# Three paired tiles at every sixth place instead of four at every fourth, with the input turned and the second half gathered earlier in each tile

## The reference, cut to what matters

```python
gate = softmax(x @ gate_w + gate_b)
topv, topi = top_k(gate, 2)                    # two of 8 experts per token
topv = topv / topv.sum(-1)
for e in range(8):
    h = relu(x @ w1[e] + b1[e])                # 256 -> 1024
    y = h @ w2[e] + b2[e]                      # 1024 -> 256
    out += y * combine[:, e]
x = layernorm(x + out)
```

## Time and profile before

| | |
|---|---|
| median of 3 runs | 1365.9 us (1363.53 to 1366.03) |
| profiled execution | 1366.0 us, of which the span from first to last instruction is 1364.2 us |
| granted TensorE clock | 0.996 of full speed |
| busy share of the span | PE 98%, DVE 77%, ACT 64%, POOL 43% |
| the chain that ended last | PE 81%, DVE 6%, issue 4%, DMA 3%, POOL 2% |

### The profile page before, as it was taken

One profiled execution on the slowest core, in us unless ns is written; L12 is line 12 of the kernel. 1 busy time (PEld: TensorE's weight loads), 2 busy tenths in 40 slices (PEclk: granted clock), 3 DMA queues, 4 the chain that ended last, 5 costly groups with the idle time before them and its releaser, 6 DMA issues.

```text
span 1364.2 us, 50089 instructions
## 1 busy us (share of the span) xinstructions
PE 1334.9 (98%) x18640; PEld 968.4 (71%) x18640; DVE 1048.9 (77%) x1997; ACT 873.0 (64%) x1927; POOL 586.2 (43%) x1046
## 2 busy tenths in 40 slices
PE   9999999999999999999999999999999999999994
PEld 5444545467776677577555556999999999998883
DVE  6888888888888888888999994677766666655654
ACT  4588888888788778778888786664322333345431
POOL 3221121222332332562222542556777776655555
PEclk9999999999999999999999999999999999999998
DMA  6336555544444423332342425333444443333331
GB/s 203 84 100 176 146 178 151 156 114 123 130 114 126 129 67 88 112 105 66 88 150 60 106 76 202 85 89 98 122 138 122 115 119 100 94 90 92 84 90 54
DMA packets 147482, 154.93 MB, mean 114 GB/s; under 512 B 67355, under 2 KB 119514, under 8 KB 146218
## 3 DMA queue, kind: packets, MB, share of 16 engines
q1 hardware_dynamic: 133082, 113.46, 30.9%
q0 software_dynamic: 13584, 36.97, 8.1%
q10 hardware_dynamic: 576, 1.31, 0.3%
HBM read 89.52 MB, written 62.13 MB: 111 GB/s over the span
## 4 chain that ended last, share of the span: by engine, by line
PE 81%; DVE 6%; issue 4%; DMA 3%; POOL 2%; SPq 2%; DVEq 1%; ACT 0%; POOLq 0%; ACTq 0%
PE pa L1183 15%; PE po L1362 15%; PE pb L1183 14%; PE pa L1444 12%; PE pb L1456 11%; PE px L1183 8%; DVE neg L1801 2%; PE pb L1176 1%; DMA space<-y_parts,y_tags 1%; PE pb L1470 1%; PE po L1176 1%; PE pa L1190 1%; PE px L1176 1%; DMA o_last<-y_parts,y_tags 1%; POOL y_parts L1115 1%
## 5 line engine op out<-in xcount | busy, mean ns | idle before, releaser
L1801 DVE TENSOR_REDUCE neg<-pa 128x1 f32<-128x1024 f32 x512 | 611.6, 1213 | 60.8 <-PE pa L1183 45.9
L1597 ACT ACTIVATE w_sb<-pb 128x512 f32<-128x512 f32 x996 | 590.9, 598 | 100.8 <-PE pb L1183 60.6
L1183 PE MATMUL pb<-w_sb 99*32 99x512 bf16 x3984 | 420.6, 380 | 2.7 <-DMA w_sb<-minus_maxima 1.4
L1183 PE MATMUL pa<-w_sb 96*32 96x512 bf16 (+1 forms) x4208 | 337.6, 379 | 3.9 <-DVE neg L1801 3.3
L1362 PE MATMUL po<-w_sb,space 128*32 128x256 f32 x4000 | 316.1, 379 | 0.1
L1718 ACT ACTIVATE space<-pa,b1T_sb 128x128 f32<-128x128 f32 x512 | 139.1, 382 | 257.8 <-PE pa L1444 257.8
L1444 PEld LDWEIGHTS pa<-xgT,attn_t 128*128 128x128 f32 x2048 | 238.8, 192 | 11.6 <-DVE xgT L2161 6.2
L1444 PE MATMUL pa<-xgT,attn_t 128*128 128x128 f32 x2048 | 242.0, 276 | 3.9 <-DVE xgT L2161 3.9
L1456 PE MATMUL pb<-w_sb,space 128*128 x1024 | 235.3, 380 | 0.0
L1456 PEld LDWEIGHTS pb<-w_sb,space 128*128 128x128 f32 x1024 | 189.0, 190 | 23.2
L1183 PEld LDWEIGHTS pa<-w_sb 96*32 96x32 bf16 (+1 forms) x4208 | 131.3, 97 | 103.6 <-DVE neg L1801 30.9
(11 more groups left out here) (305 smaller groups left out, 1340.0 us busy)
## 6 DMA issues: line engine op xcount, KB each, us to landing
y_parts<-attn_t SPq DMA_DIRECT2D x13, 896.0 KB, 5.0
w_sb<-w SPq DMA_DIRECT2D x17, 512.0 KB, 4.6
xg<-x_by_expert SPq DMA_DIRECT2D x64, 130.0 KB
attention_out<-space SPq DMA_DIRECT2D x64, 128.0 KB
w_sb<-w SPq DMA_DIRECT2D x7, 1024.0 KB, 7.1
q_parts<-w_sb SPq DMA_DIRECT2D x48, 128.0 KB, 3.1
w_sb<-q_parts SPq DMA_DIRECT2D x64, 96.0 KB, 2.6
w_sb<-k_parts SPq DMA_DIRECT2D x64, 96.0 KB, 3.3
```

What stands on the lines that cost most here:

```text
L1183: mm = pe.matmul(out[at:end], lhsT[:, at:end], rhs, start=start, stop=stop, tile_position=(0, at))
L1597: act.activation(ex_of(n)[:, half * HALF:(half + 1) * HALF], score_bank(n, half), ACT.Exp, scale=SCALE).then_inc(e_done, 1)
L1801: dve.tensor_reduce(neg[i % 2][:, t:t + 1], pa[n % 2][:, :], AX.X, ALU.max, negate=True).then_inc(max_done, 1)
```

## The change: three paired tiles, further apart, and a new order in a tile

- There are three paired tiles, at places 44, 50 and 56. `FFN_TILES` stays 68. Six odd halves go into the paired tiles; a seventh and an eighth get a tile of their own (`alone`).
- To count those tiles the last table must know the odd halves. Their count moves from `pair_tiles` into `later_tiles`, whose later steps move one tile on (tiles 18 to 21). `pair_tiles` is left with two steps, in tiles 39 and 40. The middle table's first two instructions move from tile 14 to tile 7.
- In DVE's tile `turn_x` moves ahead of `norm_3` and of the second `copy_w1`.
- In POOL's tile, from tile 12 on and not in a paired tile or the one behind it, `gather` moves ahead of `spread_3`. It gets one more wait: that the gather before it has landed.

```diff
-PAIRED = NE // 2
-FFN_TILES = 2 * NT + PAIRED
+PAIRED = 3
+FFN_TILES = 2 * NT + NE // 2
-PAIRED_AT = (50, 54, 58, 62)
+PAIRED_AT = (44, 50, 56)
-    PAIR_STEPS = 40
+    PAIR_STEPS = 39
...
+                def gathers_first(tile):
+                    return LAST_TOKENS + 1 < tile < FFN_TILES - 2 and tile not in PAIRED_AT and tile - 1 not in PAIRED_AT
+
                 def gather(tile):
...
                     if tile in PAIRED_AT:
                         pool.wait_ge(y_out[tile % TAGS], 16 * (tile // TAGS + 1))
+                    if gathers_first(tile):
+                        pool.wait_ge(x3_in, 16 * tile)
...
+                    if gathers_first(tile):
+                        gather(tile)
                     if tile:
                         spread_3(tile - 1)
...
-                    if tile < FFN_TILES - 2 and tile not in PAIRED_AT:
+                    if tile < FFN_TILES - 2 and tile not in PAIRED_AT and not gathers_first(tile):
                         gather(tile)
...
+                        if last == FFN_TILES:
+                            after("tiles")
+                            dve.scalar_tensor_tensor(odd[:, :], tiles[:, :], -2.0, half_i[:, :], ALU.mult, ALU.add).then_inc(made, 1)
...
+                            dve.scalar_tensor_tensor(alone[:, :], upto[:, :], float(2 * PAIRED), odd[:, :], ALU.is_gt, ALU.mult
+                                                     ).then_inc(made, 1)
+                            after("alone")
+                            dve.tensor_tensor(tiles[:, :], tiles[:, :], alone[:, :], ALU.add).then_inc(made, 1)
...
                         copy_w1(tile + 2, 0, e)
+                    if tile + 2 < FFN_TILES:
+                        turn_x(tile + 2)
                     if LAST_TOKENS + 1 < tile < FFN_TILES - 1 and tile - 2 not in PAIRED_AT:
                         norm_3(tile - 2)
                     if tile + 2 < FFN_TILES:
                         copy_w1(tile + 2, 1, e)
-                        turn_x(tile + 2)
...
-                    if 8 <= since < 11:
-                        later_tiles(since - 8, MIDDLE, FFN_TILES)
-                    if 0 <= tile - PAIR_STEPS < 3:
+                    if 9 <= since < 12:
+                        later_tiles(since - 9, MIDDLE, FFN_TILES)
+                    if 0 <= tile - PAIR_STEPS < 2:
```

More of the change, by code:

```diff
@@ L388, in stream @@
         slot_expert, slot_row = sb("slot_expert", [P, 1]), sb("slot_row", [P, 1])
+        half_i = sb("half_i", [P, NE], I32)
+        odd, row_of, upto, alone = (sb(n, [P, NE]) for n in ("odd", "row_of", "upto", "alone"))
         hit, found = (sb(n, [P, 2, NE]) for n in ("hit", "found"))
@@ L494, in stream @@
                  "expert_at", "left_1", "left_2", "early"]
[L495 to L499, removed]
+        TABLE_M = ["full_i", "shift", "tiles", "late", "cum", "step", "step_last", "step_tiles", "past", "expert", "weighted",
+                   "before", "row_0", "rows_128", "row_at", "expert_at", "left_1", "left_2", "left_3", "early"]
+        TABLE_2 = ["full_i", "halves", "shift", "tiles", "odd", "row_of", "upto", "alone", "wholes", "late", "cum", "step", "step_last",
+                   "step_tiles", "past", "expert", "weighted", "before", "row_0", "rows_128", "row_at", "expert_at"]
+        PAIR = ["hit_0", "hit_1", "taken", "row_hit", "row_sum", "expert_hit", "expert_sum", "free", "row_0", "expert_min", "row_64",
+                "pair_row_0", "pair_row_1", "pair_expert"]
         MADE_1, MADE_M = len(TABLE), len(TABLE) + len(TABLE_M)
@@ L2038, in later_tiles @@
                         dve.tensor_scalar(full_i[:, :], g.run[:, :], float(up_to), None, ALU.add).then_inc(made, 1)
-                    if stage == 0:
                         after("full_i")
+                        if last == FFN_TILES:
+                            dve.tensor_single_scalar(half_i[:, :], full_i[:, :], HALF_ROWS.bit_length() - 1, ALU.arith_shift_right
+                                                     ).then_inc(made, 1)
                         dve.tensor_single_scalar(full_i[:, :], full_i[:, :], P.bit_length() - 1, ALU.arith_shift_right
@@ L2044, in later_tiles @@
                         dve.tensor_copy(tiles[:, :], full_i[:, :]).then_inc(made, 1)
-                        after("tiles")
+                        if last == FFN_TILES:
+                            after("tiles")
+                            dve.scalar_tensor_tensor(odd[:, :], tiles[:, :], -2.0, half_i[:, :], ALU.mult, ALU.add).then_inc(made, 1)
+                            dve.scalar_tensor_tensor(row_of[:, :], tiles[:, :], float(P), g.step_c[:, g.col["region"]], ALU.mult, ALU.add
+                                                     ).then_inc(made, 1)
+                            after("odd")
+                            settle(dve, g.settled)
+                            dve.tensor_tensor_scan(upto[:, :], g.ones[:, 0:NE], odd[:, :], 0.0, ALU.mult, ALU.add).then_inc(made, 1)
+                            after("upto")
+                            dve.scalar_tensor_tensor(alone[:, :], upto[:, :], float(2 * PAIRED), odd[:, :], ALU.is_gt, ALU.mult
+                                                     ).then_inc(made, 1)
+                            after("alone")
+                            dve.tensor_tensor(tiles[:, :], tiles[:, :], alone[:, :], ALU.add).then_inc(made, 1)
+                    if stage == 0:
+                        after("tiles" if last < FFN_TILES else "wholes")
                         dve.tensor_tensor(tiles[:, :], tiles[:, :], early[:, :], ALU.subtract).then_inc(made, 1)
@@ L2089, in pair_tiles @@
                         dve.wait_ge(table_1, MADE_2)
[L2090 to L2104, removed]
                         for h in range(2):
-                            dve.scalar_tensor_tensor(hit[:, h, :], cum[:, :], numbers[:, h:h + 1], step[:, :], ALU.is_equal, ALU.mult
+                            dve.scalar_tensor_tensor(hit[:, h, :], upto[:, :], numbers[:, h:h + 1], odd[:, :], ALU.is_equal, ALU.mult
                                                      ).then_inc(table_1, 1)
@@ L2109, in pair_tiles @@
                         dve.tensor_reduce(taken[:, :], hit[:, :, :], AX.X, ALU.add).then_inc(table_1, 1)
-                        dve.tensor_tensor(found[:, :, :], hit[:, :, :], by_half(early[:, :]), ALU.mult).then_inc(table_1, 1)
+                        dve.tensor_tensor(found[:, :, :], hit[:, :, :], by_half(row_of[:, :]), ALU.mult).then_inc(table_1, 1)
                         after("row_hit")
@@ L2117, in pair_tiles @@
                         dve.tensor_reduce(half_expert[:, :], found[:, :, :], AX.X, ALU.add).then_inc(table_1, 1)
-                    if stage == 2:
+                    if stage == 1:
                         after("expert_sum")
```

## The result

The changed kernel takes 1356.68 us (median of 6 runs, 1354.76 to 1357.34) against 1365.47 us for the kernel before in the same comparison (6 runs, 1362.26 to 1366.03). The ratio is 0.9939, with a 95% interval from 0.9927 to 0.9951: 8.8 us faster. The forecast was 1357.9.

What follows compares the result with a forecast made beforehand. TensorE was taken to bound at 7.03 us a tile, plus paired tiles' cost and waits from the late ring POOL, DMA, DVE. Terms -4.4 - 2.4 - 1.4 + 0.1 = -8.1 us took 1366.0 to 1357.9, range 1354.7 to 1361.5.

Steps and rivals of the forecast that it cites:

- The pair and the places: U(27) to U(67): one paired tile fewer, the others six apart, late waits go, excess 6.94 to 2.56: -4.4 us.
- The tail: After U(67): with DVE no longer late, result(65) moves up 2.09 us, plus 0.3 for shorter pieces: -2.4 us.
- The transposition and the gather ahead: U(20) to U(27): 2.3 us of new room against 1.71 us of losses, 0.3 left for POOL's pace: -1.4 us.
- What costs nothing: DVE and POOL loop: later second copy is covered, the gather's new wait and later `spread_3` cost nothing.
- The tables: DVE's small table instructions, same number, moved between tiles, two more in tile 7: +0.1 us, between 0 and 0.4.
- Late again elsewhere: Rival, chance 0.13: weight copies or last tile's tags hold the end or the pairs; tail gain lost, 1361.1 us.
- only the pair: Rival, chance 0.06: lateness is not won back and waits show at the new places; 1364.4 us.
- POOL's queue: Rival, chance 0.04: in tiles 12 to 37 the moved gather leaves scatter landings open, 0.7 us a tile; 1376 us.

Runs made afterwards that it cites:

- e1: Changed kernel with both old orders (transposition behind the second copy, gather behind `spread_3`), three paired tiles kept at 44, 50, 56: 1360.32 us.
- e2: Kernel before with both new orders (gather and transposition ahead) and nothing else, four paired tiles at 50, 54, 58, 62: 1362.02 us.
- e3: Changed kernel with the transposition back behind `norm_3` and the second copy, the gather still ahead of `spread_3`: 1357.41 us.
- e4: Changed kernel with the gather back behind `spread_3`, the transposition still ahead: 1357.12 us.
- e7: Changed kernel with four paired tiles at 44, 48, 52, 56 in place of three, new orders kept: 1358.36 us.
- e6: Changed kernel with its three paired tiles moved to 50, 56 and 62, spacing still six: 1361.05 us.
- e5: Changed kernel with POOL, at tile 66, making the reciprocal root for tile 65 (`spread_3`) ahead of the gather: 1356.58 us.

## Why the prediction was right, step by step

The sum was -8.1 us; the profiled execution gave -8.7, the medians -8.8. Its mechanism, late gathers that hold up the transposition, is what the runs showed, but two of its steps leaned on the wrong part of the change, and part of the agreement is luck: the span fell by 9.7 us, 1.1 of which came from the tail and the early stretch beyond their terms, and 1.0 came back outside the span, for which the sum had no term.

**The pair and the places, -4.4: the size was right to 0.01, the reason only in part.** A paired tile cost 0.85, as read from the earlier trace rows, and the excess from U(27) to U(67) fell from 6.94 to 2.54. But the step said that six places' spacing lets four gathers win back 0.70 us each of 3.3, with the new order as an extra. The traces weigh them the other way round: of the 3.55 us of waits the places alone, with one pair less, leave 1.74 (e1), the orders alone 0.48 (e2), both together none. And in the changed kernel the lateness is not won back from one pair to the next: its gathers win 0.2, 1.35 and 1.3 us in three tiles (the rows above against 7.03), and at the next pair 1.3 us are left. What keeps TensorE from waiting is the room of 3.89 us that the earlier transposition leaves in place of 2.11, of which the pair now takes up to 2.5. With the room back at 2.10 (e3) 0.54 us stay, with it at 3.89 and the old gather (e4) none. What the spacing is worth by itself is not shown: e7, four pairs four apart, waits 1.97 us, but only behind its fourth pair, and e6, three pairs six apart, waits behind its third. Whether one pair less takes part of the waits away by itself was not tried.

**The tail, -2.4: right in its main piece, too small by 0.8 in the sum.** Result(65) moved up by the 2.09 us predicted. The pieces between result(65) and gather(66) gave 0.36, where 0.3 was allowed. Without the last step the tail would have given 2.44, as forecast. What was left out is that step: from the output of tile 66 to the last output took 4.12 us before and takes 3.35, because POOL waits 1.43 us there in place of 2.19. That wait does not go with the lateness: e6 is late and has 1.44, e7 is not late and has 1.98. It is 1.43 or 1.44 us in all six kernels with three pairs and 1.96 to 2.19 in the three with four, and the DMA packets of the stretch tell those apart. Between the issues of the last two outputs the kernel before moved (queue, kind, packets, MB, share of 16 engines)

```profile
q0 software_dynamic: 48, 0.13, 9.3%
q14 instruction: 1, 0.01, 1.0%
```

and the changed kernel

```profile
q0 software_dynamic: 48, 0.13, 11.0%
```

The output is the same 48 packets. In the three kernels with four pairs one load of 8 KB of instructions starts together with them, and the last of the 48 ends 2.54 to 2.77 us behind the output's issue. In the six with three pairs that stretch has no such load, and the last one ends at 2.13 or 2.14; the last 8 KB come after the span there, where the time around the span is longer. So the 0.77 us of this step most likely came from where a piece of the program happened to be loaded, and not from the forecast's mechanism. All nine traces agree in this, but no kernel was run that moves the load alone. Nor did the orders shorten the tail, as the step had it ("if DVE is no longer late"): the distance from the last pair to the end did. e2 and e6, with the last pair at 62, end 19.6 to 20.2 us behind U(67), the others 16.0 to 17.1.

**The transposition and the gather ahead, -1.4: measured -1.72, the upper end.** I kept 0.3 us back because POOL's 7.22 us a tile seemed to be the pace in those tiles. POOL kept that pace: the same eight tiles take 57.64 us in the changed kernel (986.38 to 1044.02). But it was not a bound: TensorE runs at 7.03 there and POOL falls behind, its gathers from 8.9 us behind U(t+1) in tile 16 to 10.4 in tile 26, which the room covers. And the 2.3 us of new room were added up from both orders, as if both were needed; e3 and e4 show that either was enough alone: the smallest room from tile 20 to 27 is 1.00 us in e3 and 1.63 in e4.

**What costs nothing.** The second copy and `spread_3` came later and TensorE waited for neither; their cover held. One wait was not foreseen. In tile 23 the transposition for tile 25, now first, waits for its blocks:

```profile
1029.54 0.45 DVE L2172 STREAM_TRANSPOSE xgT<-cv 128x256 f32<-128x256 f32 x1 [2.41 <-DMA cv<-x_by_expert]
```

It left 1.38 us of room, the smallest of all tiles behind tile 18, so it was free; any more than 1.38 us later it would have been a wait of TensorE's.

**The tables, +0.1.** No cost shows on TensorE behind U(20). Ahead of it U(20) came 0.40 us earlier, but in the changed kernel, e5 and e6, which differ only behind tile 43, it lies at 996.24, 997.12 and 997.28, so the term can't be read.

**The rivals.** *Late again elsewhere* and *only the pair* are out: no wait at the new places, and a short tail. *POOL's queue* is out too: the order it feared runs without a loss of TensorE's. The Trainium skill's rule that stood beside it ("SBUF — State Buffer", section "SBUF: two separate sides") would have a gather beside a VectorE copy wait for that copy. The trace agrees with it, at a smaller price than 0.69 us. In the changed kernel a copy runs inside gather(47), which lasts from 1203.55 to 1204.65:

```profile
1203.84 0.69 DVE L2231 COPY attn_t<-w_sb 128x1024 f32 x1 [0.44 <-issue]
```

The gather ends 0.12 us behind the copy. So does gather(27), which takes longer; it and its copy read:

```profile
1062.14 1.21 POOL L1099 DMA_INDIRECT space<-y_parts,y_tags  x1 [0.31 <-issue]
1062.46 0.77 DVE L2231 COPY attn_t<-w_sb 128x1024 f32 x1 [0.44 <-issue]
```

In the kernel before, 11 of the 14 gathers with such a copy wholly inside end 0.12 us behind it, and take 1.15 to 1.36 us; no gather of either kernel ends sooner behind one. Gathers beside no copy usually take 1.05 to 1.09. So a meeting cost up to 0.3 us; gather(47), at 0.05, is one of the cheap ones. Nor did the new place bring more of them: from 890 us on the changed kernel has 7 such meetings, the one before 14.

## What to carry to other kernels

Where a disturbance recurs in a loop, work out three things apart: how late it makes the ring, how much of that is won back before the next one, and how much lateness the bounding engine doesn't see because its input is made early in the other engine's tile. A wait on another engine is worth something only as far as it uses up the room of what the bounding engine needs next: 16.5 us of VectorE's waits were worth nothing once the earlier transposition left room for them. A disturbance near the end costs its full lateness in the tail, and there its distance from the end was worth more than the order (e1, e2, e6). And a change can move the loading of the program itself, so a wait that differs without a reason in the kernel is worth a look at the instruction queue.

## What was not expected

- The wait of POOL for the landing of the second-last output has two sizes, 1.43 to 1.44 us and 1.96 to 2.19. They go with whether 8 KB of instructions are loaded beside it, not with load or lateness of the loop.
- Gathers win back time unevenly behind a paired tile: tile 47's comes 6.87 us after the one before it, the next two 5.68 and 5.75, where the old order had 6.33.
